# Attention, layer norm and a gated low-rank layer on one core: the middle normalisation on ScalarE, two of the gate's small sums on GpSimd

## The chip, the cores and the metric

One core of a Trainium2 chip runs the whole program. The time is the device time of one execution in microseconds (us); lower is better. Five engines run side by side, each through its own instructions in their written order, and they wait for one another on semaphores: TensorE (PE), VectorE (DVE), ScalarE (ACT), GpSimd (POOL) and SyncE (SP), which issues the transfers.

## What is computed

1024 tokens (4 sequences of 256) of 512 numbers go through attention and then through a layer with a gate, each between two layer norms, with the input added behind:

```python
x = x + _layernorm(_L0_attn_ref(_layernorm(x), wq, wk, wv, wo))
x = x + _layernorm(_L0_ffn_ref(_layernorm(x), W_base, b_base, W_gate, A, B))

def _L0_ffn_ref(x, W_base, b_base, W_gate, A, B):
    result = einsum('bnd,od->bno', x, W_base) + b_base
    probs = softmax(einsum('bnd,ed->bne', x, W_gate))        # 8 experts
    top_p, top_i = top_k(probs, 2)
    top_p = top_p / sum(top_p)
    route_w = sum(one_hot(top_i, 8) * top_p[..., None], axis=-2)
    h = einsum('bnd,erd->bner', x, A)                        # rank 16
    return result + einsum('bner,eor->bno', h * route_w[..., None], B)
```

The normalisation that the change moves is the inner one of the second line, `_layernorm(x)` ahead of the gated layer. With two experts, the weights are 1/(1+g) and g/(1+g), where g = e^(second logit - first logit).

## The kernel before

The tokens are cut into 8 tiles of 128. A first part, up to about 158 us of the profiled execution, projects queries, keys and values and does the attention. The second part, which the change is in, does for each tile t: the output projection (`project_out`, 12 matmuls, each operand split in a high and a low part), its layer norm (number 1 in the arrays `stats`, `mv`, `std`, `rstd`, `nmr`) and the sum into `x_sb`; the middle layer norm (number 2) into `xn1_sb`; its transposition on TensorE (`turn_mid`) into bank 2 of the PSUM `ps`, the high part on ScalarE (`high_of_transpose`) and the rest on VectorE (`xn_l`, L903); the matmuls with `wcat`, which give the base product, the low-rank product and the 8 logits together (`base_down_router`, 24 matmuls); the gate; the gated low-rank product `hw`, turned on TensorE (`turn_hw`), copied by ScalarE (L677) and multiplied by `lora_b` (`up_projection`); the bias; the last norm (number 3), a last sum, and the store of the tile.

These stages run as a pipeline written out by hand. `tile_step(s)` of each engine does, in step s, the output projection and norm 1 of tile s, norm 2 of tile s-1 (`t1`), transposition and big matmuls of tile s-2 (`t2`), the gate of tile s-3 (`t3`), the bias and the statistics of norm 3 of tile s-4 (`t4`), and norm 3 and the output sum of tile s-5 (`t5`). Steps 0 and 1 stand within the attention part (`EARLY`), steps 2 to 12 behind it. In a step each engine's order is fixed by the code:

- VectorE: `gating_choice(t3)` (the top values, MAX8 at L847; their places; a CAST of the places to float, L850; the first selection vector, L851), `add_bias(t4)`, statistics of norm 2, `gating_weights(t3)` (L858 to L867), statistics of norm 1, `xn_l`, `ln_scale(1)`, `ln_scale(2)` and `ln_apply(2)` (L775), statistics and `ln_scale` of norm 3. `ln_scale` is a reciprocal (L767) and, for norms that ScalarE applies, a SCALAR_TENSOR_TENSOR that makes `nmr` = -mean/std (L770).
- ScalarE: `high_of_transpose(t2)` (L653), norm 3 (L636), the square roots of norms 2 and 1 (L571), norm 1 (L636, from PSUM to `z1`), the copy of the turned `hw` (L677), the square root of norm 3.
- GpSimd: the gate's difference (L503) and power (L505), the output sum (L511), the sum `x_sb` += `z1` (L516). Ahead of and between these stand four operations on 128x1024 elements: `divide(2)` ahead of step 2, `attn_low_part(2)` behind the sum of step 2, `divide(3)` behind that of step 3, `attn_low_part(3)` behind that of step 4 (L489 and L494).
- TensorE: `turn_mid(t2)`, `project_out(s)`, the first 8 matmuls of `base_down_router(t2)` (these wait for the bias sum of tile s-4, `y_ready`), `turn_hw(t3)`, the other 16, `up_projection(t3)`.

The statistics of norm 2 wait for L516 of the step before (`x1_ready`); the last step with an output projection is step 7. In the last step of the gate (10), `gating_weights` comes directly behind `gating_choice`.

## Time and profile before

| | |
|---|---|
| median of 3 runs | 239.64 us (237.5 to 241.78) |
| the profiled execution | 241.21 us |
| its span, first to last instruction | 239.4 us |
| mean granted TensorE clock | 0.986 of full speed |
| TensorE matmul busy | 205.5 us, 86% |
| VectorE busy | 165.3 us, 69% |
| GpSimd busy | 127.5 us, 53% |
| ScalarE busy | 111.9 us, 47% |

The shares are means over the whole program. The change acts in its last third only, where steps follow each other every 7.7 to 9.6 us; what decides there is read from the rows of that stretch. Where the profiled execution's own clock readings are used, 1.8 us lie outside the span (241.21 - 239.4).

### The profile page before, as it was taken

Reading aid. Unit: us, or ns where it says so; the run is one execution under the profiler, and the core shown is the slowest. Engines: PE = TensorE matmul, PEld = TensorE weight load, DVE = VectorE, ACT = ScalarE, POOL = GpSimd, SP = SyncE. Lnnn points to the kernel's source line nnn. Section 1 sums busy time; section 2 is a strip of 40 time slices with the busy share of each in tenths; the row PEclk is TensorE's granted clock in tenths of the full one; section 3 lists DMA queues with packets and bytes.
Section 4 is the critical chain, followed back from the end, with each engine's and each line's share of the span. In section 5 each row is a group of like instructions: output and inputs, shape, how many; then the busy total and the mean of one; then the engine's idle time right before and its main releaser. Section 6 shows DMA issues by size and latency. Waiting matters only on the chain.

```text
span 239.4 us, 3777 instructions
## 1 busy us (share of the span) xinstructions
PE 205.5 (86%) x1304; PEld 124.9 (52%) x1304; DVE 165.3 (69%) x342; ACT 111.9 (47%) x197; POOL 127.5 (53%) x126
## 2 busy tenths in 40 slices
PE   0599999997878699999999979889889979996870
PEld 0594834434544344445444314145768868985850
DVE  1882616778888766777777701457998898889675
ACT  2333531323023696787867775862512514433321
POOL 8200332653368596979736475883657365343332
PEclk9999999999999999999999999999999999998997
DMA  6998056986998127782932404044340010111022
GB/s 180 351 373 305 3 197 175 256 261 235 225 299 216 23 74 234 152 190 38 202 65 59 80 22 91 6 92 68 64 101 0 3 44 0 44 48 44 0 88 88
DMA packets 34065, 29.88 MB, mean 125 GB/s; under 512 B 3968, under 2 KB 29568, under 8 KB 34048
## 3 DMA queue, kind: packets, MB, share of 16 engines
q1 hardware_dynamic: 33536, 29.52, 46.1%
q10 hardware_dynamic: 512, 0.13, 0.3%
q8 instruction: 10, 0.16, 0.3%
q14 instruction: 7, 0.06, 0.1%
HBM read 17.19 MB, written 10.09 MB: 114 GB/s over the span
## 4 chain that ended last, share of the span: by engine, by line
PE 36%; DVE 26%; ACT 9%; issue 9%; DMA 7%; SPq 5%; POOL 4%; ACTq 2%; POOLq 1%; DVEq 0%
PE ps L1111 6%; DVE stats L761 5%; PE ps L1096 5%; PE ps L1070 4%; PE ps L1011 4%; ACT region_a L700 4%; PE ps L1001 3%; DVE nmax L938 3%; DVE gate L851 3%; PE ps L987 3%; DMA region_b<-q_scr 3%; PE ps L1159 3%; PE ps L1065 2%; SPq L337 2%; DMA x_sb<-x 2%
## 5 line engine op out<-in xcount | busy, mean ns | idle before, releaser
L938 DVE TENSOR_REDUCE nmax<-ps 128x4 f32<-128x1024 f32 x32 | 39.2, 1224 | 14.2 <-PE ps L1070 14.0
L524 POOL TENSOR_SCALAR_AFFINE_SELECT region_a<-region_a 128x1024 f32<-128x1024 f32 x32 | 35.3, 1108 | 19.1 <-ACT region_a L700 18.9
L700 ACT ACTIVATE region_a<-ps 128x1024 f32<-128x1024 f32 x32 | 32.8, 1024 | 0.9 <-PE ps L1096 0.8
L1096 PE MATMUL ps<-region_b,kst 98*128 98x512 bf16 x96 | 27.5, 382 | 3.5 <-ACT region_a L700 2.0
L1001 PE MATMUL ps<-region_a,region_c 128*128 128x512 f32 x64 | 29.0, 598 | 0.0
L571 ACT ACTIVATE std<-mv,eps_sb 128x1 f32<-128x1 f32 x32 | 9.3, 295 | 36.4 <-DVE mv L762 36.4
L935 DVE TENSOR_REDUCE nmax<-ps 128x4 f32<-128x512 f32 x32 | 21.9, 683 | 5.9 <-PE ps L1054 5.5
L1111 PE MATMUL ps<-region_a,v_aug 128*32 128x512 f32 x192 | 25.3, 603 | 0.6 <-POOL region_a L524 0.6
L697 ACT ACTIVATE region_a<-ps 128x512 f32<-128x512 f32 x32 | 19.2, 600 | 11.0 <-PE ps L1096 10.6
L516 POOL TENSOR_TENSOR x_sb<-x_sb,region_b 128x512 f32<-128x512 f32 x8 | 10.2, 1276 | 23.0 <-ACT region_b L636 23.0
L445 POOL TENSOR_TENSOR region_a<-region_a 128x512 f32<-128x512 f32 x4 | 6.5, 1629 | 28.4 <-DVE region_a L809 28.4
L1070 PEld LDWEIGHTS ps<-kst,region_b 96*128 96x128 bf16 x256 | 17.0, 97 | 5.6
L1070 PE MATMUL ps<-kst,region_b 96*128 96x128 bf16 x256 | 19.5, 219 | 0.0
L1001 PEld LDWEIGHTS ps<-region_a,region_c 128*128 128x128 f32 x64 | 11.6, 190 | 12.8 <-issue 12.8
L809 DVE TENSOR_TENSOR region_a<-ps,region_c 128x512 f32<-128x512 f32 x16 | 9.9, 682 | 10.4 <-PE ps L987 5.5
L761 DVE BATCH_NORM_STATS2 stats<-x_sb 128x6 f32<-128x512 f32 x16 | 11.0, 688 | 6.6 <-DMA x_sb<-x 5.7
L1096 PEld LDWEIGHTS ps<-region_b,kst 98*128 98x128 bf16 x96 | 7.5, 97 | 15.0 <-ACT region_a L700 5.0
L1065 PE MATMUL ps<-mask_bf,ident_bf 128*128 128x512 bf16 x32 | 12.3, 385 | 3.1 <-DVE nmax L938 3.0
L1050 PE MATMUL ps<-mask_bf,ident_bf 128*128 128x512 bf16 x32 | 12.3, 384 | 2.8 <-ACT mrow L709 1.1
L1159 PE MATMUL ps<-wcat_h,xn_h 128*128 128x324 f32 x64 | 11.5, 319 | 3.3 <-DVE region_b L879 1.9
L284 DVE COPY o_sb<-ps 128x512 f32<-128x512 f32 x6 | 4.1, 687 | 14.5 <-PE ps L1111 14.5
L972 PE MATMUL ps<-ident_sb,region_b 128*128 128x128 f32 x32 | 6.1, 331 | 8.4 <-DVE region_b L775 8.4
(103 smaller groups left out, 421.6 us busy)
## 6 DMA issues: line engine op xcount, KB each, us to landing
region_b<-q_scr SPq DMA_DIRECT2D x8, 768.0 KB, 6.3
q_scr<-region_c SPq DMA_DIRECT2D x8, 384.0 KB, 3.4
x_sb<-x SPq DMA_DIRECT2D x8, 256.0 KB, 6.1
q_scr<-region_c SPq DMA_DIRECT2D x8, 256.0 KB, 3.4
attn_t<-o_sb SPq DMA_DIRECT2D x32, 64.0 KB, 2.4
rden_bc<-r_scr SPq DMA_DIRECT2D x8, 256.0 KB, 3.2
out<-region_b SPq DMA_DIRECT2D x8, 256.0 KB, 2.0
kst<-k_scr SPq DMA_DIRECT2D x8, 192.0 KB, 3.9
```

The lines of the kernel that those rows point to most:

```text
L524: pool.affine_select(out=blocks, in_=blocks, compare_op=ALU.is_ge, fill=0.0, base=0, pattern=[[0, 2], [0, REP], [1, P]], channel_multiplie ...
L697: nc.scalar.activation(probs[:, u % PRING, 0, :], ps[:, 3, :], ACT.Exp, scale=float(HEAD_DIM) ** -0.5).then_inc(exp_done, 1)
L700: nc.scalar.activation(probs[:, u % PRING, 1:3, :], ps[:, 4:6, :], ACT.Exp, scale=float(HEAD_DIM) ** -0.5).then_inc(exp_done, 1)
L761: link(nc.vector.bn_stats(stats[:, k, t, :], src))
L935: nc.vector.tensor_reduce(nmax[:, gi % 2, 0, heads], ps[:, 0, :].rearrange("p (r k) -> p r k", r=REP), AX.X, ALU.max, negate=True).then_in ...
L938: nc.vector.tensor_reduce(nmax[:, gi % 2, 1, heads], ps[:, 1:3, :].rearrange("p a (r k) -> p r a k", r=REP), AX.XY, ALU.max, negate=True). ...
L1001: last = nc.tensor.matmul(ps[:, SET_BANKS[i][ri], :], wq_sb[:, c, col:col + P], xn_t[:, c, half * HALF:(half + 1) * HALF], start=(c == 0), ...
L1065: nc.tensor.matmul(ps[:, 2, :], ident_bf[:, :], mask_bf[:, :, :].rearrange("p r k -> p (r k)"), start=True, stop=False, skip_group_check=True)
L1070: last = nc.tensor.matmul(ps[:, 1 + kt, r * P:(r + 1) * P], qst[0:SROWS, slot, h, P:2 * P], kst[0:SROWS, slot, k, kt * P:(kt + 1) * P], st ...
L1096: last = nc.tensor.matmul(ps[:, 3 + j, :], kst[0:TROWS, slot, k, kt * P:(kt + 1) * P], qst[0:TROWS, slot, k * REP:(k + 1) * REP, qt * P:(q ...
L1111: last = nc.tensor.matmul(ps[32 * j:32 * j + 32, 6 + qt, :], v_aug[:, 2 * b + kt, g * GROUP_KV + j, :], probs[:, u % PRING, qt + kt, :], s ...
L1159: last = nc.tensor.matmul(ps[:, 4 + 2 * (t % 2) + hf, 0:CATH], act_part[:, t % 2, c, :], w[:, c, hf * CATH:(hf + 1) * CATH], start=(term = ...
```

## The change

Three things are moved.

- The application of norm 2 goes from VectorE (`ln_apply`, L775) to ScalarE (`normalise`), where it stands behind the two square roots and ahead of the application of norm 1. ScalarE needs `nmr` for it, so VectorE makes that for norm 2 as well, and does `ln_scale(2)` ahead of `ln_scale(1)`.
- The second selection vector (is the place the second one, times g) and the sum 1+g go from VectorE to GpSimd, behind the power; both count up `second_hot`.
- The first selection vector is no longer made by itself: VectorE's sum of both vectors becomes one SCALAR_TENSOR_TENSOR (places equal to the first, plus the second vector).

```diff
 # GpSimd, residuals(s)
                     pool.tensor_tensor(ga[:, 1:2], base_e[:, :], ga[:, 0:1], ALU.pow).then_inc(gexp_ready, 1)
+                    pool.wait_ge(gexp_ready, t3 + 1)
+                    pool.tensor_scalar(ga[:, 2:3], ga[:, 1:2], 1.0, None, ALU.add).then_inc(second_hot, 1)
+                    pool.wait_ge(index_ready, t3 + 1)
+                    pool.tensor_scalar(ga[:, 32:40], iota_sb[:, :], ga[:, 17:18], ga[:, 1:2],
+                                       ALU.is_equal, ALU.mult).then_inc(second_hot, 1)
...
 # ScalarE, tile_step(s)
                 if s < TILES:
                     sqrt(1, s)
+                if 0 <= t1 < TILES:
+                    act.wait_ge(scaled[2], t1 + 1)
+                    if t1 >= 2:
+                        act.wait_ge(xn1t_psum, t1 - 1)
+                    normalise(2, t1, xn1_sb[:, t1 % 2, :], x_sb[:, t1, :], xn1_ready)
+                if s < TILES:
                     act.wait_ge(scaled[1], s + 1)
...
 # VectorE, ln_scale(k, t)
-                if k in (0, 2):
+                if k == 0:
                     return
...
 # VectorE, gating_choice(t)
-                link(nc.vector.tensor_copy(ga[:, 16:18], gate_i[:, t % 2, 0:2]))
-                nc.vector.tensor_scalar(ga[:, 24:32], iota_sb[:, :], ga[:, 16:17], None, ALU.is_equal)\
-                    .then_inc(first_hot, 1)
+                nc.vector.tensor_copy(ga[:, 16:18], gate_i[:, t % 2, 0:2]).then_inc(index_ready, 1)
...
 # VectorE, gating_weights(t)
-                dve.wait_ge(gexp_ready, t + 1)
-                link(nc.vector.tensor_scalar(ga[:, 2:3], ga[:, 1:2], 1.0, None, ALU.add),
-                     nc.vector.tensor_scalar(ga[:, 32:40], iota_sb[:, :], ga[:, 17:18], ga[:, 1:2],
-                                             ALU.is_equal, ALU.mult))
-                dve.wait_ge(first_hot, t + 1)
+                dve.wait_ge(index_ready, t + 1)
+                dve.wait_ge(second_hot, 2 * t + 2)
                 link(nc.vector.reciprocal(ga[:, 3:4], ga[:, 2:3]),
-                     nc.vector.tensor_tensor(ga[:, 40:48], ga[:, 24:32], ga[:, 32:40], ALU.add))
+                     nc.vector.scalar_tensor_tensor(out=ga[:, 40:48], in0=iota_sb[:, :], scalar=ga[:, 16:17],
+                                                    in1=ga[:, 32:40], op0=ALU.is_equal, op1=ALU.add))
...
 # VectorE, tile_step(s)
+                if 0 <= t1 < TILES:
+                    ln_scale(2, t1)
                 if s < TILES:
                     ln_scale(1, s)
-                if 0 <= t1 < TILES:
-                    ln_scale(2, t1)
-                    if t1 >= 2:
-                        dve.wait_ge(xn1t_psum, t1 - 1)
-                    ln_apply(2, t1, xn1_sb[:, t1 % 2, :], x_sb[:, t1, :]).then_inc(xn1_ready, 1)
```

In the rows below, line numbers of the changed kernel are its own; the waits of a row stand in brackets. `region_b` holds `xn1_sb`, `z1`, `z2`, `y_sb`, `hw` and their like. ScalarE in step 6, before: the high part, norm 3, the square roots of norms 2 and 1, norm 1 from `ps`, the copy of the turned `hw`, the square root of norm 3.

```order
L653 CAST xn_h<-ps 128x512 [waits cat_psum,xn1t_psum]
L636 ACTIVATE region_b<-region_b,nmr,rstd 128x512 [waits scaled3]
L571 ACTIVATE std<-mv,eps_sb 128x1 [waits var_ready2]
L571 ACTIVATE std<-mv,eps_sb 128x1 [waits var_ready1]
L636 ACTIVATE region_b<-ps,nmr,rstd 128x512 [waits x1_ready,scaled1]
L677 COPY region_b<-ps 128x128 [waits y_psum,hwt_psum]
L571 ACTIVATE std<-mv,eps_sb 128x1 [waits var_ready3]
```

The same engine and step in the changed kernel.

```order
L659 CAST xn_h<-ps 128x512 [waits cat_psum,xn1t_psum]
L642 ACTIVATE region_b<-region_b,nmr,rstd 128x512 [waits scaled3]
L577 ACTIVATE std<-mv,eps_sb 128x1 [waits var_ready2]
L577 ACTIVATE std<-mv,eps_sb 128x1 [waits var_ready1]
L642 ACTIVATE region_b<-x_sb,nmr,rstd 128x512 [waits xn1t_psum,scaled2]
L642 ACTIVATE region_b<-ps,nmr,rstd 128x512 [waits x1_ready,scaled1]
L689 COPY region_b<-ps 128x128 [waits y_psum,hwt_psum]
L577 ACTIVATE std<-mv,eps_sb 128x1 [waits var_ready3]
```

One operation is new, the ACTIVATE from `x_sb`; norm 1, the copy of `hw` (L689, before L677) and the last square root stand behind it. GpSimd, from the sum of step 5 to that of step 6, before.

```order
L516 TENSOR_TENSOR x_sb<-x_sb,region_b 128x512 [waits z1_ready]
L503 TENSOR_TENSOR gate<-gate 128x1 [waits top_ready]
L505 TENSOR_TENSOR gate<-base_e,gate 128x1 [waits gap_ready]
L511 TENSOR_TENSOR region_b<-x_sb,region_b 128x512 [waits z2_ready]
L516 TENSOR_TENSOR x_sb<-x_sb,region_b 128x512 [waits z1_ready]
```

The same engine and place in the changed kernel.

```order
L522 TENSOR_TENSOR x_sb<-x_sb,region_b 128x512 [waits z1_ready]
L504 TENSOR_TENSOR gate<-gate 128x1 [waits top_ready]
L506 TENSOR_TENSOR gate<-base_e,gate 128x1 [waits gap_ready]
L508 TENSOR_SCALAR gate<-gate 128x1 [waits gexp_ready]
L510 TENSOR_SCALAR gate<-iota_sb,gate 128x8 [waits index_ready]
L517 TENSOR_TENSOR region_b<-x_sb,region_b 128x512 [waits z2_ready]
L522 TENSOR_TENSOR x_sb<-x_sb,region_b 128x512 [waits z1_ready]
```

Two TENSOR_SCALARs stand between the power and the output sum. VectorE in step 6, from the gate's weights to norm 2, before.

```order
L858 TENSOR_SCALAR gate<-gate 128x1 [waits gexp_ready]
L859 TENSOR_SCALAR gate<-iota_sb,gate 128x8
L862 RECIPROCAL gate<-gate 128x1 [waits first_hot,dve_chain]
L863 TENSOR_TENSOR gate<-gate 128x8
L867 SCALAR_TENSOR_TENSOR region_b<-ps,gate 128x128 [waits hwt_psum,dve_chain]
L761 BN_STATS stats<-ps 128x6 [waits wo_psum]
L762 BN_AGGR mv<-stats 128x2 [waits dve_chain]
L903 TENSOR_TENSOR xn_l<-ps,xn_h 128x512 [waits cat_psum,xn1_high]
L767 RECIPROCAL rstd<-std 128x1 [waits std_ready1]
L770 SCALAR_TENSOR_TENSOR nmr<-mv,rstd 128x1 [waits dve_chain]
L767 RECIPROCAL rstd<-std 128x1 [waits std_ready2]
L775 TENSOR_SCALAR region_b<-x_sb,mv,rstd 128x512 [waits xn1t_psum,dve_chain]
```

The same engine and place in the changed kernel.

```order
L869 RECIPROCAL gate<-gate 128x1 [waits second_hot,index_ready]
L870 SCALAR_TENSOR_TENSOR gate<-iota_sb,gate 128x8
L875 SCALAR_TENSOR_TENSOR region_b<-ps,gate 128x128 [waits hwt_psum,dve_chain]
L773 BN_STATS stats<-ps 128x6 [waits wo_psum]
L774 BN_AGGR mv<-stats 128x2 [waits dve_chain]
L911 TENSOR_TENSOR xn_l<-ps,xn_h 128x512 [waits cat_psum,xn1_high]
L779 RECIPROCAL rstd<-std 128x1 [waits std_ready2]
L782 SCALAR_TENSOR_TENSOR nmr<-mv,rstd 128x1 [waits dve_chain]
L779 RECIPROCAL rstd<-std 128x1 [waits std_ready1]
L782 SCALAR_TENSOR_TENSOR nmr<-mv,rstd 128x1 [waits dve_chain]
```

Two TENSOR_SCALARs of the gate are gone, and the sum (L863) has become a SCALAR_TENSOR_TENSOR (L870); norm 2's reciprocal stands first, now with its own `nmr`, and the TENSOR_SCALAR of 128x512 is gone.

## Rows read from the trace of the kernel before

**Rows 1.** The page's first line.

```profile
span 239.4 us, 3777 instructions
```

**Rows 2.** Windows, one a step: stretch, us, busy us (instructions) of each engine, PEclk, DMA.

```profile
172.50:181.50 9.00, 7.93 (x45) 6.77 (x44) 7.97 (x24) 2.80 (x6) 5.33 (x5) 1.00 0.33 78
181.50:190.10 8.60, 8.41 (x47) 6.93 (x46) 7.96 (x21) 2.57 (x7) 4.35 (x5) 1.00 0.01 2
190.10:199.70 9.60, 8.39 (x47) 6.89 (x45) 8.86 (x26) 3.79 (x8) 5.62 (x6) 1.00 0.07 27
199.70:207.40 7.70, 7.70 (x47) 6.99 (x46) 6.95 (x26) 3.12 (x7) 3.37 (x5) 1.00 0.09 34
207.40:215.40 8.00, 8.00 (x47) 7.04 (x46) 7.01 (x25) 3.12 (x7) 3.24 (x5) 1.00 0.10 36
215.40:224.30 8.90, 6.89 (x36) 6.22 (x35) 6.68 (x27) 2.15 (x5) 2.60 (x6) 0.81 0.08 29
```

**Rows 3.** Timeline, VectorE in step 6: start us, duration us, engine, line, operation.

```profile
199.85 0.17 DVE L847 MAX8 gate<-ps 128x8 f32<-128x8 f32 x1
...
200.53 0.23 DVE L851 TENSOR_SCALAR gate<-iota_sb,gate 128x8 f32<-128x8 f32 x1
...
201.34 0.68 DVE L761 BATCH_NORM_STATS2 stats<-x_sb 128x6 f32<-128x512 f32 x1
...
202.19 0.88 DVE L859 TENSOR_SCALAR gate<-iota_sb,gate 128x8 f32<-128x8 f32 x1
...
203.37 0.35 DVE L867 SCALAR_TENSOR_TENSOR region_b<-ps,gate 128x128 f32<-128x128 f32 x1
...
205.23 0.16 DVE L770 SCALAR_TENSOR_TENSOR nmr<-mv,rstd 128x1 f32<-128x1 f32 x1
...
205.50 0.55 DVE L775 TENSOR_SCALAR region_b<-x_sb,mv,rstd 128x512 f32<-128x512 f32 x1
...
207.50 0.17 DVE L847 MAX8 gate<-ps 128x8 f32<-128x8 f32 x1
```

**Rows 4.** Timeline, ScalarE in step 6; in brackets the idle time before.

```profile
200.85 0.82 ACT L636 ACTIVATE region_b<-region_b,nmr,rstd 128x512 f32<-128x512 f32 x1
...
205.43 0.78 ACT L636 ACTIVATE region_b<-ps,nmr,rstd 128x512 f32<-128x512 f32 x1 [0.56 <-DVE nmr L770]
...
206.10 0.26 ACT L677 COPY region_b<-ps 128x128 f32<-128x128 f32 x1
```

**Rows 5.** Timeline, GpSimd in step 6.

```profile
200.10 0.19 POOL L503 TENSOR_TENSOR gate<-gate 128x1 f32<-128x1 f32 x1 [0.18 <-DVE gate L847]
...
200.37 0.56 POOL L505 TENSOR_TENSOR gate<-base_e,gate 128x1 f32<-128x1 f32 x1
...
201.75 1.29 POOL L511 TENSOR_TENSOR region_b<-x_sb,region_b 128x512 f32<-128x512 f32 x1 [0.82 <-ACT region_b L636]
...
206.28 1.27 POOL L516 TENSOR_TENSOR x_sb<-x_sb,region_b 128x512 f32<-128x512 f32 x1 [3.24 <-ACT region_b L636]
```

**Rows 6.** Timeline, GpSimd and VectorE near 170 us, step 2.

```profile
169.12 2.39 POOL L489 TENSOR_TENSOR attn_t<-attn_t,rden_bc 128x1024 f32<-128x1024 f32 x1 [1.31 <-DMA rden_bc<-r_scr]
...
170.31 1.23 DVE L770 SCALAR_TENSOR_TENSOR nmr<-mv,rstd 128x1 f32<-128x1 f32 x1
```

**Rows 7.** Timeline, GpSimd, VectorE and TensorE in step 3.

```profile
173.67 2.39 POOL L494 TENSOR_TENSOR attn_l<-attn_t,attn_h 128x1024 fp32r<-128x1024 f32 x1
...
173.78 2.31 DVE L851 TENSOR_SCALAR gate<-iota_sb,gate 128x8 f32<-128x8 f32 x1
...
177.94 0.33 PE L1169 MATMUL ps<-ident_sb,region_b 128*128 128x128 f32 x1 [1.07 <-DVE region_b L867]
```

**Rows 8.** Timeline, VectorE and GpSimd in step 10, the gate's last.

```profile
228.19 0.17 DVE L847 MAX8 gate<-ps 128x8 f32<-128x8 f32 x1
...
229.22 1.28 POOL L511 TENSOR_TENSOR region_b<-x_sb,region_b 128x512 f32<-128x512 f32 x1
...
230.83 0.35 DVE L867 SCALAR_TENSOR_TENSOR region_b<-ps,gate 128x128 f32<-128x128 f32 x1
```

More of the change, by code:

```diff
@@ L250, in build @@
         top_ready = sem("top_ready")
-        first_hot = sem("first_hot")
+        index_ready = sem("index_ready")
+        second_hot = sem("second_hot")
         gexp_ready = sem("gexp_ready")
```

## The prediction

> **What bounds the kernel now.** The page first: the span of the profiled execution is 239.4 us [rows 1]. The change touches only the part behind the attention, so the second view is windows, one a step [rows 2]. Steps 3, 4 and 5 take 9.0, 8.6 and 9.6 us, steps 6 and 7 take 7.7 and 8.0, step 8 takes 8.9. In step 6 TensorE is busy for 7.70 of 7.70 us: that is its floor for a step with an output projection, and no faster VectorE gets below it. In step 8, which has no output projection, TensorE is busy for 6.89 of 8.90 at a granted clock of 0.81. So if everything else were free, steps 3 to 5 could give 1.3 + 0.9 + 1.9 = 4.1 us and step 7 another 0.3; that is the ceiling of what VectorE's relief can bring there.
>
> The third view is the timeline of step 6, engine by engine. VectorE goes from one MAX8 to the next in 207.50 - 199.85 = 7.65 us [rows 3], nearly TensorE's floor. Its last third is a loop over other engines: VectorE makes nmr for norm 1 at 205.23, ScalarE applies norm 1 at 205.43 (+0.20) and copies the turned hw at 206.10 (+0.67) [rows 4], GpSimd sums x_sb at 206.28, 0.85 behind ScalarE's start, for 1.27 us [rows 5].
>
> The fourth view is pairs of rows that overlap. VectorE's SCALAR_TENSOR_TENSOR on 128x1 takes 0.16 us [rows 3]; at 170.31 it took 1.23 and ended at 171.54, where GpSimd's product from 169.12 ended at 171.51 [rows 6]. The gate's TENSOR_SCALAR L851 takes 0.23 [rows 3]; at 173.78 it took 2.31 and ended 0.03 behind GpSimd's 173.67 + 2.39 [rows 7]. L859 took 0.88 from 202.19, to 203.07, GpSimd's sum 201.75 + 1.29 ended at 203.04 [rows 3, 5]. So TENSOR_SCALAR and the form with two inputs in SBUF are held until a GpSimd operation that started earlier ends. The change takes three of the first kind from a step and adds two of the second: nmr for norm 2, and the gate's sum.
>
> **The change part by part.** I count from the MAX8 of a step, "M".
>
> *VectorE, steps 6 and 7.* L851 goes (0.23, of which 0.09 overlaps the next: 0.14), and L858. The gate's reciprocal then starts at 2.34 (L859's place, 202.19 - 199.85) - 0.03 - 0.14 = M+2.17, and the gate's new sum at M+2.25. GpSimd's output sum started at M+1.90 (201.75) [rows 5]; it follows ScalarE's norm 3, which I put 0.1 earlier, so it runs from M+1.8 to M+3.07. The new sum is held by it to M+3.10 and the hw product starts at M+3.14, where it started at M+3.52 (203.37) [rows 3]. From there to the first nmr are 205.23 - 203.37 = 1.86 us, unchanged: M+5.00 in place of M+5.38. The saved 128x512 TENSOR_SCALAR (0.55, L775) lies behind it.
>
> *ScalarE.* Norm 2 from SBUF takes 0.82 [rows 4], and the next starts 0.1 before its end: 0.72. It stands ahead of norm 1. So norm 1, the copy of hw and GpSimd's x_sb sum each come 0.7 later, counted from the first nmr. Queued behind norm 2 on ScalarE is the copy, for which TensorE's up projection waits.
>
> *The loop closes on GpSimd.* From the first nmr: norm 2 at +0.20, norm 1 at +0.92, the x_sb sum at +1.77 (0.85 more), to +3.04. VectorE's nmr for norm 3 is ready to start at about +2.25, inside that sum, and has two inputs in SBUF: held to +3.07, and the next MAX8 starts 0.09 before its end, at +2.98, where it was 207.50 - 205.23 = 2.27. The period becomes 5.00 + 2.98 = 7.98 against 7.65. TensorE's floor of 7.7 hides nothing of this, since 7.98 is above it. Step 6: +0.3. Step 7 took 8.0 already: 0.
>
> *GpSimd's two new operations.* The trace has no TENSOR_SCALAR on GpSimd. Its nearest rows are the difference on 128x1, 0.19 us and 0.27 from start to start, and the power, 0.56 [rows 5]. I take the first for both, since add and compare are its kind: 0.27 + 0.25 = 0.5 us a step; the other end is the power's 0.56 for each, 0.6 more. In steps 6 and 7 the second vector is then ready at M+1.55 (power to M+1.08, 200.37 + 0.56), under VectorE's statistics, which last until M+2.17: free. If it took 0.6 more it would be at M+2.15 and would push the output sum and what it holds by 0.35.
>
> *Step 3.* Here GpSimd is late. Norm 2 can start at 171.54 + 0.04 (the held nmr of [rows 6] is now norm 2's), norm 1 at 172.3, the x_sb sum runs 173.1 to 174.4, then comes the 2.39 us of [rows 7] to 176.75 (before: 176.06), then difference, power and the two new ones (0.27 + 0.6 + 0.5) to about 178.0. The hw product starts 0.25 later, 178.25; before it was 0.40 ahead of TensorE's 177.94, 177.54 [rows 7]. That is +0.7, and the copy behind two norms is another +0.7: step 3 ends 1.4 later. What L851's 2.31 us give back is lost here, since VectorE waits for GpSimd's vector instead.
>
> *Step 4.* x_sb sum and the 2.39 us product stand in a row again, then the gate's chain. The delay of 1.4 is handed on, the longer chain adds a little: 1.5 at its end.
>
> *Step 5.* The last 2.39 us operation waits for a cast on ScalarE that stands behind both norms; it comes 0.9 later, and the CAST of the places (a 2.31-us hold was L851's) waits for it now. The bias sum, on which TensorE's big matmuls wait, is 0.8 late, then the output sum holds the gate's new sum, then the copy is late: about +2.0 at the end of step 5.
>
> *Steps 8 to 10.* Step 8 has no norm 1: hw at M+3.14 for M+3.52, -0.4. Step 9: GpSimd has no sum in the way, the two TENSOR_SCALARs save -0.3. Step 10: before, the hw product started 230.83 - 228.19 = 2.64 behind MAX8 [rows 8]. Now the second vector is ready at +1.55, GpSimd goes straight on to its output sum (its input was ready before the 229.22 of [rows 8]), 1.5 to 2.79, the new sum is held to 2.82 and hw starts at 2.86: +0.2.
>
> **Sum:** 2.0 (to step 5) + 0.3 (step 6) + 0 (step 7) - 0.4 - 0.3 + 0.2 = **+1.8 us**: 241.2 for this execution becomes 243.0. The execution stands 1.6 us above the median of 239.64, to which I add the same: **241.4 us**.
>
> **The rivals.**
>
> *1. The new sums are not held.* The gate's sum at M+2.25 could start ahead of GpSimd's, or a 128x8 operation could pass. The Trainium skill ("SBUF — State Buffer", Who interferes with whom) says that whoever of the two starts first has the shared ports for the whole instruction and the other blocks fully; by its rule it is the order of issue alone that decides here, and [rows 6] agree with it (held from 170.31 to 171.54). A new sum that passes is worth 3.14 - 2.44 = 0.7 us in steps 5 to 8 and 0.9 in step 10, cut by TensorE's floor of 7.7 in steps 6 and 7 (0.3 each): in all 0.7 + 0.3 + 0.3 + 0.4 + 0.9 = 2.6 us, so 1.8 - 2.6 = -0.8: 238.8 us. Against it: the lead of GpSimd is 0.45 us in steps 6 and 7. 16%.
>
> *2. All of VectorE's relief arrives.* GpSimd's chain in steps 3 to 5 would have to be hidden. Then -4.1 (steps 3 to 5) - 0.3 - 0.4 - 0.3 - 0.9 = -6.0: 233.6 us. Against it is the arithmetic of step 3, which needs only the 2.39-us row. 3%.
>
> *3. Slower by more: the GpSimd TENSOR_SCALARs with per-partition scalars are dear.* Each excess e on the pair counts in full in steps 3, 4, 5, 9 and 10 and less 0.25 in steps 6 to 8. With the power's 0.56 each, e = 0.6: 5 x 0.6 + 3 x 0.35 = +4.0, so +5.8: 245.4 us. It passes 2% (+4.8) from e = 0.47. 14%.
>
> *4. TensorE's clock.* In step 8 the granted clock averaged 0.81 [rows 2], behind a step in which TensorE was kept waiting; step 3 waited 1.07 us and kept 1.00 [rows 2, 7]. The changed step 3 lets it wait 1.8 and more. One more fall of the size of step 8's would be 0.19 x 8.9 = 1.7 us: +3.5, 243.1 us. 15%.
>
> **How the numbers follow.** The sum as worked out has 52%, the rivals 16, 3, 14 and 15. The predicted time is 241.4. The range, from rival 1 to nearly rival 3, is 238.4 to 245.2. Two per cent, about what a measurement of this kernel can tell from no change, is 4.8 us: faster than 234.8 only by rival 2 (0.03); slower than 244.4 by most of rival 3 and a part of rival 4 (0.17); within, 0.80.
>
> **What would show it.** Right: in step 6, VectorE's SCALAR_TENSOR_TENSOR for the gate taking about 0.9 us and ending with GpSimd's output sum; nmr for norm 3 taking 0.8 or more and ending with GpSimd's x_sb sum; VectorE idle in step 3 from 175 to 178 ahead of the gate's reciprocal; the copy of hw two norms behind the first nmr. Wrong: GpSimd's two new operations far from 0.2 us each, TensorE without gaps in steps 4 to 7, or a granted clock below 1 in steps 3 to 7.

## The result, and the profile after

| | before | changed |
|---|---|---|
| median, run side by side | 238.94 us (4 executions) | 242.84 us (4 executions, 241.07 to 243.63) |
| once more on another chip | 239.25 us (23) | 243.21 us (4, 243.08 to 243.38) |
| the profiled execution, first chip | 241.21 us | 242.87 us |

The ratio is 1.0148 with a 95% interval of 1.0081 to 1.0216, and 1.0154 (1.01 to 1.0208) the second time. The forecast of 241.4 us was 1.4 too low, inside its range of 238.4 to 245.2, on the right side of no change. The change costs 3.5 us by the ratio and 3.9 by the medians (3.7 and 4.0 the second time), where the sum said 1.8. Ratios and intervals, here and below, leave out executions more than 1.5% above the fastest of their kernel; medians take all.

The page of the changed kernel, first line, which answers [rows 1]:

```profile
span 241.0 us, 3777 instructions
```

Its windows, one a step from step 3 to step 8, answer [rows 2]; the columns are the same (stretch, us, then PE, PEld, DVE, ACT and POOL busy, PEclk, DMA).

```profile
172.00:181.50 9.50, 7.13 (x40) 5.93 (x38) 3.92 (x17) 3.79 (x8) 5.02 (x6) 1.00 0.29 72
181.50:192.00 10.50, 9.50 (x51) 7.91 (x52) 7.03 (x22) 4.09 (x9) 6.20 (x7) 1.00 0.01 2
192.00:202.00 10.00, 8.52 (x47) 6.81 (x46) 8.75 (x23) 3.72 (x8) 6.15 (x8) 1.00 0.07 26
202.00:210.10 8.10, 8.03 (x47) 7.03 (x46) 6.98 (x23) 3.72 (x8) 3.98 (x7) 1.00 0.09 32
210.10:218.20 8.10, 8.00 (x47) 7.03 (x46) 6.97 (x23) 3.72 (x8) 3.96 (x7) 1.00 0.09 34
218.20:225.50 7.30, 5.56 (x36) 4.91 (x35) 5.79 (x23) 2.75 (x6) 3.31 (x8) 1.00 0.10 37
```

VectorE is busy for 8.4 us less over the program (156.9 for 165.3), ScalarE for 5.4 more and GpSimd for 5.3 more. The difference shows above all in step 3 (3.92 us busy for 7.97, of which 2.31 were L851 being held), and there it is idle time; in steps 6 and 7 it is as busy as before, 6.98 for 6.95, and the next view says why. Step 8 ran at a granted clock of 1.00, where before's ran at 0.81.

The timeline of step 6 in the changed kernel (start us, duration us, engine, line, operation) answers [rows 3], [rows 4] and [rows 5]. VectorE first:

```profile
202.09 0.16 DVE L859 MAX8 gate<-ps 128x8 f32<-128x8 f32 x1
...
204.20 1.12 DVE L870 SCALAR_TENSOR_TENSOR gate<-iota_sb,gate 128x8 f32<-128x8 f32 x1
205.35 0.35 DVE L875 SCALAR_TENSOR_TENSOR region_b<-ps,gate 128x128 f32<-128x128 f32 x1
...
207.21 0.16 DVE L782 SCALAR_TENSOR_TENSOR nmr<-mv,rstd 128x1 f32<-128x1 f32 x1
...
209.46 0.79 DVE L782 SCALAR_TENSOR_TENSOR nmr<-mv,rstd 128x1 f32<-128x1 f32 x1
210.18 0.16 DVE L859 MAX8 gate<-ps 128x8 f32<-128x8 f32 x1
```

GpSimd in the same step:

```profile
203.28 0.23 POOL L508 TENSOR_SCALAR gate<-gate 128x1 f32<-128x1 f32 x1
203.48 0.42 POOL L510 TENSOR_SCALAR gate<-iota_sb,gate 128x8 f32<-128x8 f32 x1
204.00 1.29 POOL L517 TENSOR_TENSOR region_b<-x_sb,region_b 128x512 f32<-128x512 f32 x1
208.97 1.27 POOL L522 TENSOR_TENSOR x_sb<-x_sb,region_b 128x512 f32<-128x512 f32 x1 [3.68 <-ACT region_b L642]
```

ScalarE in the same step:

```profile
207.41 0.82 ACT L642 ACTIVATE region_b<-x_sb,nmr,rstd 128x512 f32<-128x512 f32 x1 [0.56 <-DVE nmr L782]
208.13 0.76 ACT L642 ACTIVATE region_b<-ps,nmr,rstd 128x512 f32<-128x512 f32 x1
208.79 0.25 ACT L689 COPY region_b<-ps 128x128 f32<-128x128 f32 x1
```

The gate's new sum takes 1.12 us and ends at 205.32, 0.03 behind GpSimd's output sum (204.00 + 1.29 = 205.29). `nmr` for norm 3 takes 0.79 and ends at 210.25, 0.01 behind the `x_sb` sum (210.24). Both are VectorE operations with two inputs in SBUF, held by a GpSimd operation that started first. The period, from MAX8 to MAX8, is 210.18 - 202.09 = 8.09 us for 7.65.

Step 3 of the changed kernel, TensorE, GpSimd and VectorE in order of time, against [rows 7]:

```profile
173.60 2.42 POOL L495 TENSOR_TENSOR attn_l<-attn_t,attn_h 128x1024 fp32r<-128x1024 f32 x1
...
177.12 0.42 POOL L510 TENSOR_SCALAR gate<-iota_sb,gate 128x8 f32<-128x8 f32 x1
177.64 0.16 DVE L869 RECIPROCAL gate<-gate 128x1 f32<-128x1 f32 x1 [3.04 <-POOL gate L510]
...
178.37 0.33 PE L1174 MATMUL ps<-ident_sb,region_b 128*128 128x128 f32 x1 [2.08 <-DVE region_b L875]
...
181.70 0.54 PE L1178 MATMUL ps<-lora_b_sb,region_b 128*128 128x324 f32 x1 [0.49 <-ACT region_b L689]
```

VectorE stands idle for 3.04 us until GpSimd's second vector is there. Behind the 2.42-us operation, difference, power and the two new operations take until 177.54. TensorE waits 2.08 us for `hw`, where it waited 1.07, and 0.49 more for the copy that now stands behind two norms.

Step 2 went the other way. GpSimd and VectorE there, against [rows 6]:

```profile
168.35 2.39 POOL L490 TENSOR_TENSOR attn_t<-attn_t,rden_bc 128x1024 f32<-128x1024 f32 x1 [0.53 <-DMA rden_bc<-r_scr]
...
170.31 0.44 DVE L782 SCALAR_TENSOR_TENSOR nmr<-mv,rstd 128x1 f32<-128x1 f32 x1
```

VectorE no longer applies norm 2 there, the product starts 0.77 us earlier (0.2 of this the two profiles already differ by at 157 us, ahead of anything that the change touches), and `nmr` takes 0.44 us for 1.23. So VectorE's MAX8 of step 3 stands at 171.75, for 172.81 before.

### The profile page after: what moved, and what is told of

It is laid out like the page before. It is cut to its first block, busy times and chain, and to the rows that moved or that the text cites. A ratio compares the mean times of both kernels' runs of the same rounds, so it can differ in the third digit from the quotient of the medians.

```text
span 241.0 us, 3777 instructions
## 1 busy us (share of the span) xinstructions
PE 203.9 (85%) x1304; PEld 122.5 (51%) x1304; DVE 156.9 (65%) x318; ACT 117.3 (49%) x205; POOL 132.8 (55%) x142
## 4 chain that ended last, share of the span: by engine, by line
PE 34%; DVE 18%; issue 12%; POOL 11%; ACT 10%; DMA 7%; SPq 5%; ACTq 2%; POOLq 1%; DVEq 0%
PE ps L1116 6%; PE ps L1101 5%; PE ps L1075 4%; ACT region_a L712 4%; PE ps L1016 3%; DVE stats L773 3%; PE ps L1006 3%; DVE nmax L943 3%; POOL attn_l L495 3%; PE ps L992 3%; DMA region_b<-q_scr 3%; SPq L338 3%; PE ps L1070 2%; POOL x_sb L522 2%; DMA x_sb<-x 2%
## 5 line engine op out<-in xcount | busy, mean ns | idle before, releaser
L600 ACT CAST region_c<-region_a 128x512 bf16<-128x512 f32 x8 | 4.7, 618 | 18.3 <-DVE region_a L829 17.2
```

## The experiments

All kernels were profiled and timed beside the kernel before. "Period" is the time from one MAX8 of the gate to the next, and "hw" the start of VectorE's `hw` product behind MAX8. Where TensorE's part counts, a step is taken from one `turn_mid` to the next. The theory under test is the chain that the prediction worked out: the new sums are held by GpSimd, the gate's chain stands behind the 2.4-us operations, and the copy of `hw` stands behind two norms. The rivals lay the loss on the new GpSimd operations themselves, or on TensorE's granted clock.

### Each part alone

The norm alone on the kernel before:

```diff
 # before + ScalarE, tile_step: norm 2 ahead of norm 1; VectorE: no ln_apply, ln_scale(2) first, nmr for norm 2
-                if k in (0, 2):
+                if k == 0:
                     return
```

> The kernel before with one part of the change: norm 2 applied by ScalarE ahead of norm 1; the gate stays as it was. Theory 1 (the loss comes from norm 2 standing ahead of norm 1 on ScalarE: the copy of the turned hw and the x_sb sum come 0.7 us later, and nmr for norm 3 is held by that sum): slower than before by 2.5 to 3.5 us, the period of steps 6 and 7 about 8.3 us (hw product at 3.5 behind MAX8 as before, first nmr at 5.4, next MAX8 3.0 later), nmr for norm 3 taking 0.8. Theory 2 (GpSimd's longer gate chain costs it all): within 0.5 us of before.

Measured: 243.68 us for 239.61, ratio 1.0174 (1.0131 to 1.0218). The periods of steps 6 and 7 are 8.32 and 8.34 us, hw stays at 3.50 and 3.52. The timeline of its step 6, GpSimd and then VectorE:

```profile
209.84 1.26 POOL L516 TENSOR_TENSOR x_sb<-x_sb,region_b 128x512 f32<-128x512 f32 x1 [3.94 <-ACT region_b L636]
```

```profile
210.34 0.78 DVE L776 SCALAR_TENSOR_TENSOR nmr<-mv,rstd 128x1 f32<-128x1 f32 x1
```

`nmr` ends 0.02 behind GpSimd's sum here too, with the gate as before: this hold is the work of the norm alone. The norm's move by itself brings a loss as large as the whole change's, and more than the 2.5 to 3.5 us expected. The mean granted clock of its executions, 0.986 to 0.994, is that of the kernel before (0.986 to 0.994 in all but one of its 17 executions). So a loss of this size needs no fall of the clock. Its timeline shows only a part of it in the steps: GpSimd's last 128x1024 operation ahead of the second part starts at 159.12 us for 157.55, so 1.57 us of the difference of the two profiles lie ahead of anything that the edit touches.

The gate alone on the kernel before:

```diff
 # changed kernel with norm 2 back on VectorE
-                if k == 0:
+                if k in (0, 2):
                     return
```

> The kernel before with the other part: the second selection vector and the sum on GpSimd, norm 2 still applied by VectorE. Theory 1: 0 to 1 us faster than before: the gate's hw product 3.2 to 3.3 behind MAX8 in steps 5 to 7 for 3.5, steps 6 and 7 at TensorE's floor of 7.7; in step 3 the hw product is later by the two added operations, 0.1 to 0.4. Theory 2: 2.5 to 3.5 us slower, with the loss in steps 3 to 5.

Measured: 241.73 us, ratio 1.0124 (1.0067 to 1.0181): 2.1 us slower by the medians, 3.0 by the ratio. Theory 1, with 0 to 1 us faster, missed it; theory 2 had 2.5 to 3.5 us slower, but put the loss in steps 3 to 5, where the profile shows 0.9. Steps 6 and 7 are as theory 1 said: periods 7.38 and 7.55, for 7.65 and 8.07 before. Steps 3 and 5 are slower, 8.53 us for 8.01 and 10.05 for 9.61. The timeline of step 5, GpSimd and then VectorE:

```profile
194.79 0.41 POOL L510 TENSOR_SCALAR gate<-iota_sb,gate 128x8 f32<-128x8 f32 x1
195.16 1.26 POOL L517 TENSOR_TENSOR region_b<-x_sb,region_b 128x512 f32<-128x512 f32 x1
```

```profile
195.30 0.16 DVE L863 RECIPROCAL gate<-gate 128x1 f32<-128x1 f32 x1 [2.62 <-POOL gate L510]
195.38 1.07 DVE L864 SCALAR_TENSOR_TENSOR gate<-iota_sb,gate 128x8 f32<-128x8 f32 x1
```

VectorE waits 2.62 us for the vector, and then, the output sum having followed at once, its own sum is held by that (1.07 us). TensorE waits 1.88 us there. The profiled execution kept a granted clock of 1.00 in steps 3 to 8, but over the six executions the mean clock was 0.964 to 0.990; the four at 240.6 to 241.7 us had 0.983 to 0.990 and the two at 243.8 and 244.1 had 0.971 and 0.964. The two parts' losses in the medians (4.1 and 2.1 us) are more than the change's 3.5 to 4.0. In the profiles, where all four kernels kept a granted clock of 1.00 in steps 3 to 7, the parts add up (`turn_mid` to `turn_mid`, us, and the difference to before):

| | before | norm alone | gate alone | changed |
|---|---|---|---|---|
| step 3 | 9.29 | +1.04 | +0.50 | +1.72 |
| step 4 | 8.57 | +0.71 | -0.08 | +0.63 |
| step 5 | 9.63 | +0.02 | +0.43 | +0.48 |
| steps 6 and 7 | 15.70 | +0.98 | -0.22 | +0.47 |
| sum | 43.19 | +2.75 | +0.63 | +3.30 |

The norm's move is most of it. In steps 6 and 7 the gate's part takes a little back: hw comes 0.25 earlier, and the periods are 8.09 for 8.32.

### The output sum waits for hw

```diff
 # changed kernel, GpSimd, residuals(s)
                     pool.wait_ge(z2_ready, t5 + 1)
+                    if t3 < TILES:
+                        pool.wait_ge(hw_ready, t3 + 1)
```

> The changed kernel with GpSimd's output sum waiting for the step's hw product, so that it can't hold the gate's new sum. If the hold of the new sum (0.75 to 1.1 us in five steps) is on the path: the new sum takes 0.2, the hw product starts 2.4 behind MAX8 for 3.2, the last gate step gives 0.8, steps 6 and 7 come down to 7.7: 1.5 to 3 us faster than the changed kernel. If it is hidden: within 0.5 of it.

Measured: 240.76 us (12 executions, 240.1 to 242.06), ratio 1.0068 (1.0041 to 1.0095), 2.4 us below the eight executions of the changed kernel (median 243.1), 2.0 by the ratios. Step 6 of its timeline, VectorE and GpSimd:

```profile
200.20 0.78 DVE L784 SCALAR_TENSOR_TENSOR nmr<-mv,rstd 128x1 f32<-128x1 f32 x1
200.91 0.16 DVE L861 MAX8 gate<-ps 128x8 f32<-128x8 f32 x1
...
203.01 0.21 DVE L872 SCALAR_TENSOR_TENSOR gate<-iota_sb,gate 128x8 f32<-128x8 f32 x1
```

```profile
203.75 1.29 POOL L519 TENSOR_TENSOR region_b<-x_sb,region_b 128x512 f32<-128x512 f32 x1 [1.05 <-DVE region_b L877]
```

The new sum takes 0.21 us for 1.12, hw starts at 203.25, 2.34 behind MAX8 (3.26 before this edit), and the period is 7.87 for 8.09: with `nmr` still held (0.78) and TensorE's floor at 7.7, 0.22 of the 0.92 is left. The periods of steps 5 to 8 give 0.88 + 0.22 + 0.21 + 0.38 = 1.7 us, step 10's earlier hw (2.22 for 3.09) another 0.9. Rival 1 of the prediction had put this hold at 2.6 us; the sizes agree, and the hold was there and on the path.

### Norm 2 behind norm 1 and the copy

```diff
 # changed kernel, ScalarE, tile_step(s)
-                if 0 <= t1 < TILES:  ... normalise(2, t1, ...)      # ahead of norm 1
...
                     nc.scalar.copy(hw_t[:, t3 % 2, :], ps[:, 3, 0:P]).then_inc(hwt_ready, 1)
+                if 0 <= t1 < TILES:  ... normalise(2, t1, ...)      # here
 # VectorE: ln_scale(1, s) ahead of ln_scale(2, t1)
```

> The changed kernel with norm 2 on ScalarE behind norm 1 and the copy of hw, and its scale on VectorE behind that of norm 1. Theory 1: the copy and the x_sb sum are back at their old distance from the first nmr (0.87 and 1.05), nmr for norm 3 takes under 0.3, steps 6 and 7 fall from 8.08 to 7.7 us, step 3 shortens by 1.2 or more: 2 to 3 us faster than the changed kernel, level with before within 1 us. Theory 2: no faster than the changed kernel by more than 0.5.

Measured: 243.94 us, ratio 1.0146 (1.0077 to 1.0215), no faster than the changed kernel, where 2 to 3 us had been expected. The schedule did what was expected of it where GpSimd is not late: periods of 8.03 and 7.75 us, hw at 2.66 and 2.38, no hold. But step 5 took 10.61 us and step 8 8.40. TensorE's timeline in step 5:

```profile
195.79 0.33 PE L1173 MATMUL ps<-ident_sb,region_b 128*128 128x128 f32 x1 [1.94 <-DVE region_b L874]
195.87 2.19 PE L1163 MATMUL ps<-wcat_l,xn_h 128*128 128x324 f32 x8
197.87 2.17 PE L1163 MATMUL ps<-wcat_h,xn_l 128*128 128x324 f32 x8
```

And the windows of that stretch (PEclk stands behind POOL's count):

```profile
194.00:196.00 2.00, 0.21 (x2) 0.21 (x3) 1.76 (x4) 0.00 (x0) 1.32 (x2) 1.00 0.00 0
196.00:198.00 2.00, 2.00 (x10) 2.00 (x10) 1.90 (x8) 0.85 (x2) 0.00 (x0) 0.56 0.35 131
198.00:200.00 2.00, 2.00 (x10) 2.00 (x9) 0.78 (x4) 1.27 (x4) 1.28 (x1) 0.58 0.00 0
```

Behind a wait of 1.94 us the granted clock goes from 1.00 (2.4 GHz) to about a half (1.2 GHz), and groups of 8 matmuls take 2.19 and 2.17 us where the kernel before took 1.43. In step 8 the clock fell once more (0.80 over the step), behind a wait of 1.03 us. The miss pointed to a second price of TensorE's waits beside their own length, which the filled kernel below tests. A repeat of the same kernel:

> The changed kernel with norm 2 behind norm 1 and the copy of hw once more, beside its filled twin. Expected as in the first run: the schedule of steps 3, 4, 6 and 7 shorter than the changed kernel's, the mean granted clock 0.972 to 0.982 in most executions, 243 to 244 us.

Measured: 243.05 us for 239.25, ratio 1.0102 (1.0035 to 1.0168), again with a 1.94-us wait in step 5 and 2.48 us for the second group of 8 behind it. Step 8, with the same wait of 1.03 us, kept a clock of 1.00 this time and took 7.16 us for 8.69.

### Matmuls that fill TensorE's waits

Matmuls of constants into a part of PSUM that nothing reads, ahead of `turn_hw`, keep TensorE busy while it waits for hw. They add work and take none away.

```diff
 # norm 2 behind (as above); counts {3: 4, 5: 9, 8: 5} for steps 3, 5, 8
+                for _ in range(counts.get(s, 0)):
+                    nc.tensor.matmul(ps[:, 3, P:4 * P], ident_bf[:, :], mask_bf[:, 0:3, :]..., start=True, stop=True)
                 if 0 <= t3 < TILES:
                     turn_hw(t3)
```

> The same kernel with matmuls that do no work of the kernel's (128x384 bf16 into unused columns of bank 3) in TensorE's waits for the hw product in steps 3, 5 and 8, some 0.7, 1.5 and 0.8 us of them. If the time that this kernel lacks was lost to TensorE's clock falling behind its waits: clock 0.985 or more in most executions, no stretch of steps 3 to 8 under 1.00, 1.5 to 3 us faster than the twin without them. If the clock falls for another reason (total load, temperature of the chip): the same clock and time, or later by what the matmuls take.

Measured: 240.71 us (12 executions), ratio 1.0038 (1.0002 to 1.0074), 2.3 us below its unfilled twin, 1.5 by the ratios. Nine of the twelve had a mean granted clock of 0.983 to 0.987, where the twins had 0.964 to 0.983; two had 0.974, and one, at 249.91 us, 0.952. TensorE in step 5:

```profile
194.50 1.64 PE L1198 MATMUL ps<-mask_bf,ident_bf 128*128 128x384 bf16 x9
196.60 0.33 PE L1173 MATMUL ps<-ident_sb,region_b 128*128 128x128 f32 x1 [0.46 <-DVE region_b L874]
196.69 1.43 PE L1163 MATMUL ps<-wcat_l,xn_h 128*128 128x324 f32 x8
```

The wait is down to 0.46 us and the 8 matmuls take 1.43. The filler speeds up nothing but the clock, so the fall of the clock behind the waits cost this kernel some 1.5 to 2.3 us. The two profiles show one such fall: step 5 takes 10.12 us for the twin's 11.55, so 1.4 us a fall. Steps 3 to 7 of the filled kernel take 43.18 us, before's 43.19 and the changed kernel's 46.49: with norm 2 behind and the clock kept up, the 3.3 us are gone.

### nmr by TENSOR_SCALAR, bare and filled

```diff
 # changed kernel, VectorE, ln_scale(k, t)
-                nc.vector.scalar_tensor_tensor(out=nmr..., in0=mv..., scalar=-1.0, in1=rstd..., op0=ALU.mult, op1=ALU.mult)
+                nc.vector.tensor_scalar(nmr..., mv..., rstd..., -1.0, ALU.mult, ALU.mult)
```

> The changed kernel with nmr made by a TENSOR_SCALAR on 128x1 (mean times 1/std, a per-partition scalar, times -1) in place of the form with two inputs in SBUF. If the hold comes from the second input in SBUF: nmr for norm 3 takes 0.13 to 0.2 in steps 4 to 7 for 0.79, MAX8 starts 0.6 earlier behind the first nmr, steps 6 and 7 take 7.7 to 7.8 us for 8.08, 1 to 2 us faster than the changed kernel at the same granted clock. If GpSimd holds any VectorE operation there: 0.8 as before, no change.

Measured: 243.23 us for 240.36 (10 executions), ratio 1.0115 (1.0067 to 1.0163). GpSimd and VectorE at the end of its step 6:

```profile
208.01 1.26 POOL L522 TENSOR_TENSOR x_sb<-x_sb,region_b 128x512 f32<-128x512 f32 x1 [3.52 <-ACT region_b L642]
```

```profile
208.51 0.21 DVE L782 TENSOR_SCALAR nmr<-mv,rstd 128x1 f32<-128x1 f32 x1
```

This form takes 0.21 us in the midst of GpSimd's sum: it isn't held. The gate's new sum isn't held either then (hw starts 2.58 behind MAX8), and the periods of steps 6 and 7 go from 8.09 to 7.93, not to the 7.7 to 7.8 expected. TensorE's floor of 7.7 and the copy behind two norms remain. Step 8 loses much of this again: the gate's sum is held there for 1.10 us in all, and the period is 6.95 for 6.39. So the MAX8 of step 10 stands 1.1 us earlier than in the changed kernel, and by the ratios the kernel is 0.8 to 0.9 us faster, a little under the 1 to 2 expected; its median of 243.23 is that of the changed kernel, but the kernel before was slower on this chip too (240.36). In nine of ten executions the mean granted clock was 0.978 to 0.980. In the profiled one it fell in step 3, behind a wait of 1.86 us (8 matmuls took 2.34). The same kernel with filler in steps 3, 5 and 8 ({3: 9, 5: 6, 8: 5}):

> The changed kernel with nmr by TENSOR_SCALAR and the same filling in steps 3, 5 and 8 (1.5, 1.0 and 0.8 us). The unfilled one ran at a mean clock of 0.979 with a fall in step 3. If the waits bring the fall: 0.985 or more, and 1.5 to 2.5 us faster than the unfilled one's 243.2, which shows the gain that its schedule had promised. Else 243 again.

Measured: 242.29 us, ratio 1.0118 (1.0082 to 1.0153). The clock came back (0.985 to 0.991 in nine of ten), the median came down by 0.9 and the ratio not at all (1.0118 for 1.0115). So the expected gain of 1.5 to 2.5 us did not come: the fall in step 3 is cheap. The timelines say why. From `turn_mid` to `turn_mid` step 3 took 11.56 us without filler and 10.75 with it, but step 4 8.42 and 9.25: GpSimd's 2.4-us operation and its gate chain set the end of step 4 whether TensorE arrives early or late.

### The changed kernel again

> The changed kernel itself on this chip, to set the others beside: 1.0 to 2.0% slower than the kernel before, clock near 0.987.

Measured: 243.21 us, ratio 1.0154 (1.01 to 1.0208). This profile caught the fall that the first did not, in step 3, behind a wait of 2.09 us:

```profile
178.00:180.00 2.00, 1.11 (x6) 1.11 (x7) 1.77 (x6) 0.30 (x1) 0.06 (x1) 0.83 0.02 4
180.00:182.00 2.00, 2.00 (x9) 2.00 (x8) 0.69 (x5) 1.47 (x3) 0.00 (x0) 0.50 0.00 0
```

Step 3 took 11.65 us from `turn_mid` to `turn_mid` for 11.01 in the first profile, but step 4 8.53 for 9.20: 20.18 us for 20.21 in the two together. MAX8 of step 8 stood at 218.77 for 218.26, but this 0.5 us stood already at the `turn_mid` of step 3 (172.19 for 171.66), ahead of the fall. Of the fall itself nothing is left, as in `nmr_single`.

### GpSimd's long operations behind the gate's chain

```diff
 # changed kernel, GpSimd, residuals(s): in steps 3, 4, 5, behind power and the two new operations
+                if 0 <= t3 < TILES and s in (3, 4, 5):
+                    pool.wait_ge(hw_ready, t3 + 1)
+                between()          # attn_low_part(2), divide(3), attn_low_part(3)
                 if 0 <= t5 < TILES - 1:
                     pool.wait_ge(z2_ready, t5 + 1)
+                    if t3 < TILES:
+                        pool.wait_ge(hw_ready, t3 + 1)
...
-                if s == 3:  divide(BATCH - 1)
-                if s in (2, 4):  attn_low_part(BATCH - 3 + s // 2)
```

> The changed kernel with GpSimd's three 128x1024 operations of steps 2 to 4 (the low part, the product, the low part) put behind the gate's chain of the next step, and behind a wait for the hw product, which the output sums get too. Theory 1 (in steps 3 to 5 VectorE waits for a gate chain that is queued behind these 2.4 us): the hw product starts 2.2 to 4 us behind MAX8 in step 3 for 6.2, about 2.4 in step 4 for 5.9 and 2.4 in step 5 for 5.3; steps 3 to 5 take 26 us or less for 30.3; 3 to 5 us faster than the changed kernel at the same granted clock. If the steps are bound otherwise (TensorE, the attention's values): less than 1 us.

Measured: 236.68 us for 240.36 (4 executions), ratio 0.9849 (0.9768 to 0.9929). GpSimd in its step 3:

```profile
175.20 0.41 POOL L510 TENSOR_SCALAR gate<-iota_sb,gate 128x8 f32<-128x8 f32 x1
176.48 2.40 POOL L495 TENSOR_TENSOR attn_l<-attn_t,attn_h 128x1024 fp32r<-128x1024 f32 x1 [0.86 <-DVE region_b L877]
```

The second vector is ready at 175.61, 1.9 us earlier than in the changed kernel, and TensorE no longer waits for hw in step 3; it waits 1.32 us for the copy there. Steps 3 to 5 take 25.8 us (`turn_mid` to `turn_mid`) for 30.3, a gain of 4.5. That and the 2.4 us of the output sum's hold, less its share of 0.9 in step 5, which is in both, make 6.0 of the 6.5 us between this kernel and the changed one. That is more than the 3 to 5 us expected.

### All of it, with the change and without

`all_four` is the changed kernel with norm 2 behind, `nmr` by TENSOR_SCALAR, the long operations behind the gate and the output sums behind hw. `before_rest` is the kernel before with the last three, and neither part of the change.

> The changed kernel with all four edits: norm 2 behind norm 1 and the copy, output sums behind the hw product, nmr by TENSOR_SCALAR, the long operations behind the gate. At full clock steps 4 to 7 at TensorE's floor of 7.7, step 8 about 6.0: the span 3 to 5 us shorter than before's, 234 to 237 us. If TensorE's clock falls in it as in the kernel with norm 2 behind (0.972 for 0.99), 2 to 3 us of that are lost again: level with before.

> The kernel before (neither part of the change) with the three other edits: nmr by TENSOR_SCALAR, the long operations behind the gate and the hw product, output sums behind the hw product. What the change itself is worth once its side effects are gone is this against the one with all four: VectorE has 0.5 us more of a step here but stays within TensorE's floor of 7.7. Expected: within 1 us of the one with all four, steps 4 to 7 at 7.7.

Measured: `all_four` 234.25 us (231.96 to 236.36), ratio 0.9717 (0.9642 to 0.9793). `before_rest` 234.02 us (232.78 to 235.35), ratio 0.9753 (0.9694 to 0.9812). The window of step 6 of `all_four`, and then of `before_rest`:

```profile
194.75:202.45 7.70, 7.70 (x47) 6.97 (x46) 5.67 (x22) 3.63 (x10) 3.90 (x7) 1.00 0.18 68
```

```profile
193.10:200.80 7.70, 7.70 (x47) 6.98 (x46) 6.95 (x27) 3.12 (x7) 3.45 (x5) 1.00 0.15 57
```

Both go at TensorE's floor there and in the steps around it (7.73 to 7.75 us from one `turn_mid` to the next in steps 3 to 7), without a wait, and both are some 6 us below the kernel before and 9 below the changed one. VectorE is busy for 1.3 us less in `all_four` (5.67 for 6.95), and nothing comes of it: with its side effects gone, `all_four` is 0.2 us behind by the medians and 0.9 ahead by the ratios, both inside the intervals, which are 1.4 us or more to either side. So what the change itself is worth here is not told apart from nothing.

## Why the prediction was right, and where it was short

The sum was made against the profiled execution; against it the steps stand as follows (MAX8 to MAX8, changed less before, us).

| | predicted | measured in the two profiles |
|---|---|---|
| ahead of the MAX8 of step 3 | 0 (not looked at) | 171.75 - 172.81 = -1.06 |
| steps 3 to 5 | +2.0 | 30.34 - 27.04 = +3.30 |
| step 6 | +0.3 | 8.09 - 7.65 = +0.44 |
| step 7 | 0 | 8.08 - 8.07 = +0.01 |
| step 8 | -0.4 | 6.39 - 8.04 = -1.65 |
| step 9 | -0.3 | 4.64 - 4.58 = +0.06 |
| step 10 (hw) | +0.2 | 3.09 - 2.64 = +0.45 |
| sum | +1.8 | +1.55 |

**What held.** The loop of step 6, each link: hw at M+3.26 (3.14 was worked out), from the first `nmr` to the next MAX8 2.97 us (2.98), period 8.09 (7.98), both holds with the GpSimd operation that was named for them. In step 3 VectorE stood idle ahead of the reciprocal as said. In step 5 the CAST of the places was held as said, 2.01 us. `d_sum_waits` shows the hold of the gate's sum to be on the path, `long_behind_gate` the queue on GpSimd, and `norm_behind_filled` the place of norm 2 on ScalarE. The hold of `nmr` is there in each profile, but its price by itself is not shown: `nmr_single`, which takes it away, loses the gate's hold with it, and `d_sum_waits`, which keeps it, has periods of 7.87. Rivals 1 and 2 are out: the sums were held, and of VectorE's relief only that of step 2 arrived. Step 5 in the changed kernel, GpSimd and VectorE:

```profile
192.05 2.40 POOL L495 TENSOR_TENSOR attn_l<-attn_t,attn_h 128x1024 fp32r<-128x1024 f32 x1
...
195.93 1.28 POOL L517 TENSOR_TENSOR region_b<-x_sb,region_b 128x512 f32<-128x512 f32 x1
```

```profile
192.46 2.01 DVE L862 CAST gate<-gate_i 128x2 f32<-128x2 uint32 x1
...
196.15 1.08 DVE L870 SCALAR_TENSOR_TENSOR gate<-iota_sb,gate 128x8 f32<-128x8 f32 x1
```

**Luck.** The profiles' +1.55 for the sum's +1.8 is no confirmation of its size. The prediction took step 2 as it was before, norm 2 starting behind the hold of [rows 6]. It overlooked that step 2 gets shorter, and so had the start of the `x_sb` sum at 173.1 and the end of the long operation behind it at 176.75; they stood at 172.35 and 176.02. The hw product came at 177.97, near the forecast 178.25, since GpSimd's chain and what VectorE does behind it took 0.3 us longer than was put down for them. Steps 3 to 5 cost 3.3 us in place of 2.0, and what step 2 gave back hid it: +2.2 at the MAX8 of step 6. Two more errors cancel, the next one below and the fall of the clock in step 8 of the kernel before.

**A term mis-sized.** GpSimd's two new operations were put at 0.27 + 0.25 us. The 128x1 one takes 0.23; the 128x8 one takes 0.42, and from the end of the power to the end of the second vector pass 203.90 - 203.18 = 0.72. The vector is ready at M+1.81, not M+1.55 (which should have read 1.08 + 0.52 = M+1.60, as 176.75 and the 1.37 us of step 3's chain make 178.1 and not 178.0). That is dear in three places. In steps 6 and 7 the output sum starts when GpSimd itself is free (204.00 = M+1.91) and not when ScalarE's norm 3 is done (M+1.8): +0.1 each. In step 9 hw waits for the vector, so the 0.3 that was to be saved is lost. In step 10 the sum starts at 231.06 = M+1.77, and hw is 0.2 later than forecast, against [rows 8]:

```profile
232.38 0.35 DVE L875 SCALAR_TENSOR_TENSOR region_b<-ps,gate 128x128 f32<-128x128 f32 x1
```

In these steps that is +0.2 (steps 6 and 7) + 0.4 (step 9) + 0.2 = +0.8. Rival 3, which had the same thing at an excess of 0.6 us, is right in kind at 0.2.

**The step that failed** is the last one, from the execution to the median: "The execution stands 1.6 us above the median of 239.64, to which I add the same". The profiled execution of before had a fall of the clock in step 8 that the profiled one of after did not have. Step 8 took 8.84 us from `turn_mid` to `turn_mid`, and `a_norm_only`, with the same gate at a clock of 1.00, took 7.42, so the fall cost 1.4 us. (Rival 4 priced it at 1.7 and put it down to the step ahead, but [rows 2] have TensorE busy for 8.00 of 8.00 us there; its waits of 1.24 and 0.77 us are in step 8 itself.) The changed kernel's profiled execution, 242.87, lies at its median. So the profiles differ by 1.66 us and the medians by 3.9: the offset of 1.6 us was a property of that one execution of before, and the changed kernel's does not have it.

At a full clock the timelines account for 3.2 us: step 3 begins 0.39 us earlier, counted from GpSimd's last 128x1024 operation ahead of 160 us, steps 3 to 7 cost 3.30, step 8 gives 0.26 (7.16 for 7.42) and steps 9 and 10 cost 0.51. The second profile of the changed kernel gives 3.8 in the same way, since its step 2 was longer. The measured 3.5 to 4.0 us hardly need more than these; the intervals (1.9 to 5.2 us, 2.4 to 5.0) could not tell more. Rival 4, a further fall of the clock, is shown for the kernels with norm 2 behind (some 1.4 us a fall), but for the changed kernel the one fall that was caught, in step 3, left nothing.

**Still open.** Why `b_gate_only` is 2.1 us slower than before: its profile accounts for some 0.7, and its executions have a lower clock (0.964 to 0.990), but it wasn't run with filler. And why the loss of `a_norm_only`, 4.1 us (3.1 to 5.2 by its interval), is that of the whole change: its profile accounts for 2.3, and the 1.57 us that it lies behind ahead of the second part are those of one execution; the part ahead of the change differs by up to 2.4 us between the profiles of this case (that operation starts at 156.74 to 159.12).

## What to carry to other kernels

Work that is taken off an engine is worth what the engine's wait ends on: here VectorE's relief turned into idle time behind GpSimd in steps 3 and 4 (3.04 and 2.39 us), and into holds by GpSimd in steps 5 to 8. Before small operations are moved to GpSimd, look at what long operation stands ahead of them and at which of its operations will overlap a two-input operation on VectorE; here moving three long operations behind the gate's chain and the output sums behind `hw` was, with `nmr` in its other form, worth some 6 us on the kernel before, and the change itself nothing that could be measured. When a sum over steps comes out right in total, compare it step by step: here errors of 0.8 to 1.3 us cancelled. When a difference is worked out from one profiled execution, compare its granted clock step by step with what is usual before the difference is added to a median.

## What the runs showed of the hardware

- The granted clock fell to its lower level (1.2 GHz, 0.50 of full) in the midst of a busy stretch behind single TensorE waits of 1.86, 1.94 (twice) and 2.09 us, and in step 8 behind waits of 1.24 and 0.77 us (the kernel before) and of 0.68 and 1.03 us (`c_norm_behind`): 8 matmuls then took 2.1 to 2.5 us for 1.43, for the next 3 to 4 us. It didn't behind the changed kernel's wait of 2.08 us in its first profile, `d_sum_waits`'s 1.95 or `b_gate_only`'s 1.88, nor behind the same 0.68 and 1.03 us in `norm_behind_again`. A fall cost 1.4 us where TensorE set the step (steps 5 and 8) and nothing where GpSimd did (step 3).
- Of VectorE's forms on tiny tiles, SCALAR_TENSOR_TENSOR on 128x1 was held by GpSimd (0.79 us), and so were the CAST of 128x2 (2.01) and TENSOR_SCALAR on 128x8 (2.31, [rows 7]); TENSOR_SCALAR on 128x1, with a scalar from SBUF, was not (0.21 us). The Trainium skill ("SBUF — State Buffer", Who interferes with whom) says that two SBUF inputs contend with a GpSimd operation that reads SBUF, and that cast and TENSOR_SCALAR can, when their operands meet the conditions of a mode with two ports: the traces agree, down to this tile of 128x2, and show that a 128x1 tile of the second passes. The kernel before has it too, with an immediate: L858 at 194.78 took 0.12 us inside GpSimd's sum of 194.10 to 195.39. The prediction's "TENSOR_SCALAR and the form with two inputs in SBUF are held" was too wide by this form.
- GpSimd's TENSOR_SCALAR takes 0.23 us on 128x1 with an immediate, and 0.42 on 128x8 with two scalars from SBUF: 0.2 us apart for seven more columns and another kind of scalar, which no run took apart.
